# Packed biases for all keys of the second half of the queries, and copies and value products in other places, in a two-layer attention kernel

## The chip, the cores and the metric

The kernel runs on one core of a Trainium2 chip (trn2). The metric is the time of the device from the start to the end of one execution, in microseconds; several executions are timed and their median is taken.

## What is computed

Four images of 32 x 32 tokens with 768 channels pass through two layers. Both normalise over 32 groups of 24 channels, attend with 12 heads of 64 channels, project, and add the result to the input. Cut to what matters:

```python
# layer 0: every query sees all 1024 keys, with a bias by row and one by column
x = group_norm(x); q, k, v = x @ Wq + bq, x @ Wk + bk, x @ Wv + bv
attn = q @ k.T / 8
attn = attn + rel_bias_h[:, :, :, :, None] + rel_bias_w[:, :, :, None, :]
x = x + (softmax(attn) @ v) @ Wp + bp
# layer 1: every query sees its 7 x 7 neighbourhood (clipped at the borders)
x = x + neighbourhood_attention(group_norm(x), qkv_w) @ out_w
```

## The kernel before

Everything is in single precision. A matmul operand that needs it is split into a rounded part (hi) and the rest (lo), and three passes (hi by hi, hi by lo, lo by hi) stand for one product. There are eight phases f: layer 0 and layer 1 of each image. A phase projects q and k (in `project`), then v, then runs over six pairs p of heads, and ends with the output projection.

**Units.** In layer 0 a pair has 16 units u. Unit u takes the tile t = u % 8 of 128 keys and the half u // 8 of 512 queries, for both heads. `scores` issues the passes of a unit, each as two matmuls of 64 rows (head 0 on the upper half of the array, head 1 on the lower): three for q and k, then the bias. The bias is a product of a 0/1 matrix that tells each key's row and column (`onehot`, 64 lines) with the bias of each query (b_hi, then b_lo): two passes, k = 3 and k = 4. A packed unit needs one pass for both: `packed` holds of b_hi and b_lo only the lines that the keys at hand use, side by side, and `key_block` is the 0/1 matrix for it. Before the change a packed unit must lie in the upper half of the key tiles (t >= 4), and from u = 4 (6 in pair 0) or u = 12 on. Head by head the maxima of the next pair (L1327, two passes, DVE reduces them) are woven into the units. ScalarE (ACT) takes the exponential of a unit's scores into one of six `prob` slots (L828), GpSimd (POOL) adds the units up into `acc` for the denominators (L644), and TensorE (PE) multiplies prob with v (`values`, L1453), four units at a time (`GROUPED`), and sums `acc` over partitions (`sums`, L1470). `scores` of a unit waits for the exponential of the unit two before it. The order of all of it is written out by hand in each engine's program; engines meet at semaphores.

**Queue of SP.** All DMAs of the pairs are issued in one queue, in this order for a pair p > 0 of layer 0: `load_bias` for pair p + 2; `spread(p - 1, 1)`, eight DMAs that spread the reciprocals of the second half of pair p - 1 over the partitions (L491), waiting for DVE's reciprocal (L1016), which waits for ACT's copy of the sums (L734), which waits for the sums (L1470) that PE issues after unit 1; in the last pair the weights of chunk 9; `pack(p, 1)`, twelve DMAs into `packed1` (L475 and L477, four times two of rows and one of columns); `spread(p, 0)`; `pack(p + 1, 0)`, twelve DMAs into `packed0`. In pair 0 `pack(0, 0)` and `pack(0, 1)` stand behind each other when v is ready. PE waits for the twelve DMAs in front of pass k = 3 of the first packed unit of a half:

```python
if is_packed and u in PACKED_FROM[p > 0] and k == 3:
    pe.wait_ge(pack_in[half], packed_no(f, p))
```

**Layer 1.** A pair has 8 units, one for each tile of keys, over 224 to 352 queries. `values` of units 4 to 7 of the pair before come behind unit 1 and those of units 0 to 3 behind unit 5; `sums` of the pair before follow unit 3 and `shift` (L1370) of the next pair follows unit 5. ACT copies the pair's output (L728, `out_copy`) after the exponential of unit 2.

**Start.** `WARM_UP` products of ones (L1478) run before the first statistics, then PE waits for the first normalised input.

Of the kernel before, what the change touches and what calls it, by code (L numbers as in the profile page):

```python
# [33 lines left out]
ADDS = (2 * QT - 2, QT - 2)  # L34
PARTS = (2, 1)
GROUPED = 4
WARM_UP = 6
ORDER = (list(range(QT)), [0, 7, 1, 6, 2, 5, 3, 4])
P_SLOTS = 6
LAST = PAIRS - 1  # L40
# [1 line left out]
SET_LOADS = [128 + 16, 0, 128, 128]  # L42
G_SLOTS = 3
BLOCK = SIDE // 2
PACKED_FROM = ([6, 12], [4, 12])


def centre(i):
# [141 lines left out]
    return 192 * (f // 2 * PAIRS + p + 1)  # L190


def first_no(f, p):

    return f // 2 * (PAIRS + 1) + (PAIRS + 1 if f % 2 else p + 1)
# [22 lines left out]
def rows_of(h):  # L218
    return slice(64 * h, 64 * h + 64)
# [17 lines left out]
def build(nc, x_in, w_in, bqk_in, bv_in, bp_in, rel_in, onehot_src, block_in, mask_in, group_src, ident_in,  # L237
# [53 lines left out]
    for s, at in enumerate(bias_at):  # L291
# [4 lines left out]

    packed = [m.put("packed0", [128, 2, HALF], F32R, at=slot_at[0]),
              m.put("packed1", [128, 2, HALF], F32R, at=one + 40 * KB)]  # L300
    max_wide0 = m.put("max_wide0", [128, 4, 256], F32R, at=slot_at[0] + 8 * KB)

    onehot_raw = m.put("onehot_raw", [128, TOKENS], at=m.at)
# [45 lines left out]
    turned, b_first, max_mm, max_ok, col_ok, shift_mm = (sem(n) for n in (  # L349
        "turned", "b_first", "max_mm", "max_ok", "col_ok", "shift_mm"))  # L350
    half_mm, half_max_ok, wide_ok = sem("half_mm"), sem("half_max_ok"), sem("wide_ok")
    onehot_in, onehot_ok, pack_in = sem("onehot_in"), sem("onehot_ok"), sems("pack_in", 2)
    shifted, b_hi_ok, b_lo_ok = sem("shifted"), sem("b_hi_ok"), sem("b_lo_ok")
    score_ok, prob_ok, pv_done, added, acc_zero = (sem(n) for n in (
        "score_ok", "prob_ok", "pv_done", "added", "acc_zero"))
# [52 lines left out]
    with nc.Block() as block:  # L408

        @block.sync  # L410
        def _(sp):
# [24 lines left out]
            def load_bias(f, p):  # L436
                s = SET_OF[f % 2][p]
                if p == 0:
                    sp.wait_ge(gshift_ok, norm_no(f, len(norm_parts(f)) - 1))
                elif p == 1:  # L440
                    sp.wait_ge(v_mm, f * VN + 2 * QT)
                elif p > 2:
                    sp.wait_ge(score_ok, unit_no(f, p - 3, 2 * QT - 1))
                    sp.wait_ge(pack_in[1], packed_no(f, p - 3))
                else:
                    sp.wait_ge(v_mm, (f + 1) * VN)
                if f % 2:
                    sp.dma_start(b_lo_raw[s][:, :], mask_in).then_inc(bias_in[s], 16)
                    return
                sp.wait_ge(g_sent[p % G_SLOTS], 16 * (f // 2 * 2 + p // G_SLOTS + 1))  # L450
                for h in range(2):
                    for part, dst in ((0, b_lo_raw[s]), (1, b_hi_raw[s])):
                        a = 64 * h + SIDE * part
                        band = bass.AP(g_mem[p].tensor, ((p * 2 + h) * 128 + 64 * part) * TOKENS,
                                       [[TOKENS, SIDE], [TOKENS + SIDE, SIDE], [1, SIDE]])
                        sp.dma_start(dst[a:a + SIDE, :].rearrange("p (i j) -> p i j", j=SIDE), band)\
                            .then_inc(bias_in[s], 16)

            def pack(f, p, h):


                s = SET_OF[0][p]
                sp.wait_ge(b_lo_ok, f // 2 * PAIRS + p + 1)
                if p:
                    sp.wait_ge(score_ok, unit_no(f, p - 1, (h + 1) * QT - 1))
                else:
                    sp.wait_ge(v_mm, (f + 1) * VN)
                cols = slice(h * HALF, (h + 1) * HALF)
                to = packed[h][:, :, :].bitcast(F32)
                for e, part in enumerate((b_hi[s], b_lo[s])):  # L470
                    for head in range(2):
                        a, b = 64 * head, 64 * head + BLOCK * e
                        for n in range(2):
                            rows = part[a + BLOCK * n:a + BLOCK * n + BLOCK, cols].bitcast(F32)
                            sp.dma_start(to[b:b + BLOCK, n, :], rows).then_inc(pack_in[h], 16)  # L475
                        columns = part[a + SIDE:a + SIDE + BLOCK, cols].bitcast(F32)
                        sp.dma_start(to[b + SIDE:b + SIDE + BLOCK, :, :],  # L477
                                     columns.unsqueeze(1).to_broadcast([BLOCK, 2, HALF]))\
                            .then_inc(pack_in[h], 16)

            def load_onehot(f):
                sp.dma_start(onehot_raw[:, :], onehot_src[f % 2]).then_inc(onehot_in, 16)
# [21 lines left out]
            for f in range(PHASES):  # L504
# [38 lines left out]
                for p in range(PAIRS):  # L543
                    if layer == 1:
                        if p == 3:
                            if f + 1 < PHASES:
                                sp.wait_ge(bn_ok, 2 * (f + 2) * CT)
                            weights(f, 9)
                        if p == LAST and f + 1 < PHASES:
                            sp.wait_ge(shifted, pair_no(f, LAST))  # L550
                            sp.dma_start(group[:, :, :], group_src).then_inc(group_in, 16)
                        if p:
                            spread(f, p - 1, 0)
                        if p == 0:
                            next_tile(3)
                            next_tile(4)
                        if p == 1:
                            next_tile(5)
                        continue
                    if 0 < p < PAIRS - 2:  # L560
                        load_bias(f, p + 2)
                    if p:
                        spread(f, p - 1, 1)
                    if p == LAST:
                        sp.wait_ge(pack_in[1], packed_no(f, LAST - 1))
                        weights(f, 9)
                    if p:
                        pack(f, p, 1)
                    if p == LAST:
                        sp.wait_ge(score_ok, unit_no(f, LAST, QT - 1))  # L570
                        weights(f, 10)
                    spread(f, p, 0)
                    if p < LAST:
                        pack(f, p + 1, 0)
# [102 lines left out]
        def _(act):  # L677
# [74 lines left out]
            for f in range(PHASES):  # L752
# [67 lines left out]
                for p in range(PAIRS):  # L820
                    for u in range(UNITS[layer]):
# [8 lines left out]
                        if layer == 0:  # L830
# [12 lines left out]
                            if u == 9:  # L843
                                if ahead:
                                    bias_turn(f, p + 2, 1)
                                sums_copy(f, p, 0)
                            if u == 10 and ahead:
                                bias_first(f, p + 2)
                            if u == (11 if p else 13) and p < LAST:
                                widen(f, p + 1)  # L850
                            if u == 12:
                                out_copy(f, p, 0)
                            if u == (12 if p else 13) and p < LAST:
                                bias_hi(f, p + 1)
                        else:
                            if u == 2 and p:
                                out_copy(f, p - 1, 0)
                            if u == 3 and p:
                                sums_copy(f, p - 1, 0)
# [389 lines left out]
        def _(pe):  # L1249
# [126 lines left out]
            def scores(f, p, u, n=None):  # L1376
# [4 lines left out]
                keys = slice(t * 128, (t + 1) * 128)  # L1381
                ug = units_before(f, p) + u
                half = u // QT
                is_packed = layer == 0 and t >= QT // 2 and u >= PACKED_FROM[p > 0][half]
                passes = 4 if layer or is_packed else 5

                def score_pass(k, h):
                    w = (k_hi, k_hi, k_lo, None, None)[k]
                    x = (q_hi, q_lo, q_hi, b_hi[s], b_lo[s])[k]
                    if k < 3:  # L1390
                        w, x = w[rows_of(h), p, keys], x[rows_of(h), p, a:b]
                    elif is_packed:
                        w, x = key_block[rows_of(h), t % 2, :], packed[half][rows_of(h), int(t % 4 < 2), :]
# [5 lines left out]
                def bias_ready(k):  # L1399
                    if is_packed and u in PACKED_FROM[p > 0] and k == 3:  # L1400
                        pe.wait_ge(pack_in[half], packed_no(f, p))
                    if u == 0 and k == 3:
                        pe.wait_ge(shifted, pair_no(f, p))
                        if layer == 0:
                            pe.wait_ge(b_hi_ok, f // 2 * PAIRS + p + 1)
# [66 lines left out]
                sums_issued[0] += 1  # L1472


            pe.wait_ge(const_ok, 1)
            one_column = ones[:, 0:1]
            for n in range(WARM_UP):
                nc.tensor.matmul(score[:, 0, 0, :], one_column.to_broadcast([128, 128]),  # L1478
                                 one_column.to_broadcast([128, HALF]), start=True, stop=True)
            mean_averages(0, 0)  # L1480
            shift_averages(0, 0)
            for f in range(PHASES):
                layer = f % 2
                hi, lo = in_halves(f)
# [65 lines left out]
                for p in range(PAIRS):  # L1550
                    for u in range(UNITS[layer]):
                        if layer == 1:
                            scores(f, p, u)
                            if u == GROUPED + 1:
                                for e in range(GROUPED):
                                    values(f, p, e)
                            elif u == 1 and p:
                                for e in range(QT - GROUPED, QT):
                                    values(f, p - 1, e)
                            if u == 3 and p:  # L1560
                                sums(f, p - 1, 0)
                            if u == 5 and p < LAST:
# [18 lines left out]
                            sums(f, p - 1, 1)  # L1581

                last_pair = PAIRS - 1
                for u in range(UNITS[layer] - GROUPED, UNITS[layer]):
                    values(f, last_pair, u)

                def output(n, c):
# [113 lines left out]
```

## Time and profile before

| | |
|---|---|
| median of 3 runs | 3190.11 us (3186.83 to 3190.49) |
| the profiled execution, its own time | 3189.31 us |
| its span, first to last instruction | 3187.5 us |
| mean granted clock of TensorE | 0.997 |
| busy: PE, DVE, ACT, POOL | 98%, 54%, 38%, 34% |
| layer 0's pair, from its first unit to the next pair's | 42.8 us in pairs 1 to 3 |
| layer 1's pair | 12.45 us |

PE is the engine to read first, since it is nearly always busy. The table gives the length of a pair because the change works inside a pair: there are 24 of each layer.

### The profile page before, as it was taken

The page shows a single profiled execution, that of the slowest core. Times are in us where ns is not written, and L with a number is a line of the kernel's source. Part 1 is how long each engine was busy: PE and PEld are TensorE (multiplying, and loading weights), DVE is VectorE, ACT ScalarE, POOL GpSimd, SP SyncE. Part 2 cuts the span into 40 slices and gives each one's busy share as a digit, 9 for nine tenths or more (in the row PEclk, how much of TensorE's full clock was granted, in tenths as well). Part 3 has the DMA queues.
Part 4 walks back from the last instruction along what each step waited for, and adds up shares of the span by engine and source line. Part 5 has one row for each costly group of instructions (what it writes and reads, how often), then busy time and mean ns, then how long its engine had stood idle before and what let it go on. Part 6 is the DMA issues. An engine that isn't in the chain of part 4 may idle for free.

```text
span 3187.5 us, 48944 instructions
## 1 busy us (share of the span) xinstructions
PE 3113.8 (98%) x20072; PEld 2319.8 (73%) x20072; DVE 1719.5 (54%) x1921; ACT 1223.3 (38%) x1397; POOL 1086.1 (34%) x618
## 2 busy tenths in 40 slices
PE   8999999999999999999999999999999999999999
PEld 6876558887787555888778755688777875568876
DVE  4448745436435884444734588444463457744434
ACT  3345542134234654213423465321342355532132
POOL 0037860025003776003400487500430057840042
PEclk9999999999999999999999999999999999999999
DMA  3212223114321223211531222411153122141113
GB/s 128 94 39 51 47 79 116 40 57 143 133 94 32 51 46 99 98 40 65 170 123 67 40 49 43 133 69 41 63 179 109 67 47 51 38 138 60 41 34 116
DMA packets 193178, 249.38 MB, mean 78 GB/s; under 512 B 123200, under 2 KB 135872, under 8 KB 192960
## 3 DMA queue, kind: packets, MB, share of 16 engines
q1 hardware_dynamic: 191424, 244.69, 26.1%
q8 instruction: 163, 2.67, 0.4%
q10 hardware_dynamic: 1536, 1.57, 0.2%
q14 instruction: 55, 0.45, 0.0%
HBM read 145.50 MB, written 50.33 MB: 61 GB/s over the span
## 4 chain that ended last, share of the span: by engine, by line
PE 81%; ACT 5%; POOL 5%; issue 4%; DVE 3%; DMA 1%; SPq 0%; ACTq 0%; POOLq 0%
PE score L1251 14%; PE score L1252 13%; PE score L1253 13%; PE lot L1453 12%; PE score L1396 12%; PE lot L1327 8%; POOL acc L644 5%; ACT prob L828 2%; PE lot L1470 2%; DMA raw<-weights 1%; PE lot L1251 1%; PE lot L1253 1%; PE lot L1252 1%; PE lot L1370 1%; PE lot L1294 1%
## 5 line engine op out<-in xcount | busy, mean ns | idle before, releaser
L644 POOL TENSOR_TENSOR acc<-acc,prob 128x1024 f32<-128x1024 f32 x288 | 714.0, 2479 | 181.4 <-ACT prob L828 147.2
L828 ACT ACTIVATE prob<-score 128x1024 f32<-128x1024 f32 (+3 forms) x576 | 516.0, 910 | 391.6 <-PE score L1396 388.1
L974 DVE TENSOR_REDUCE max_part<-lot 128x1 f32<-128x512 f32 x640 | 412.0, 685 | 130.9 <-PE lot L1327 124.9
L1453 PE MATMUL lot<-prob,v 128*64 128x512 f32 (+4 forms) x2496 | 463.9, 515 | 8.7 <-ACT o_raw L724 7.1
L644 POOL TENSOR_TENSOR acc<-prob 128x1024 f32<-128x1024 f32 x48 | 120.1, 2503 | 833.1 <-ACT prob L828 833.1
L1396 PE MATMUL score<-q_hi,k_hi 64*128 64x512 f32 (+3 forms) x1152 | 340.7, 406 | 23.1 <-ACT prob L828 20.9
L1327 PE MATMUL lot<-k_hi,q_hi 64*128 64x512 f32 (+2 forms) x1152 | 335.7, 393 | 10.3 <-issue 5.4
L1453 PEld LDWEIGHTS lot<-prob,v 128*64 128x64 f32 x2496 | 166.9, 138 | 236.1 <-issue 197.2
L895 DVE TENSOR_TENSOR w_lo<-raw,w_hi 128x1536 fp32r<-128x1536 f32 x95 | 181.8, 1914 | 247.4 <-ACT w_hi L681 247.0
L1396 PE MATMUL score<-q_lo,k_hi 64*128 64x512 f32 (+3 forms) x1152 | 309.4, 359 | 0.0
L1396 PE MATMUL score<-q_hi,k_lo 64*128 64x512 f32 (+3 forms) x1152 | 309.1, 359 | 0.0
L662 POOL COPY acc<-prob 128x256 f32<-128x256 f32 x96 | 41.0, 428 | 752.7 <-ACT prob L828 695.6
L1327 PE MATMUL lot<-onehot,b_hi 64*128 64x512 f32 x768 | 259.4, 390 | 0.0
L681 ACT ACTIVATE w_hi<-raw 128x1536 fp32r<-128x1536 f32 x96 | 142.5, 1484 | 295.0 <-DMA raw<-weights 295.0
L1251 PE MATMUL score<-in_b,w_hi 128*128 128x512 f32 x576 | 228.3, 396 | 12.0 <-DVE in_a L951 6.4
L960 DVE TENSOR_REDUCE max_col<-lot 128x2 f32<-128x448 f32 (+1 forms) x192 | 139.7, 770 | 185.8 <-PE lot L1327 185.8
L1396 PEld LDWEIGHTS score<-q_hi,k_hi 64*128 64x128 f32 x1152 | 154.7, 184 | 114.6 <-ACT prob L828 75.2
L1327 PEld LDWEIGHTS lot<-k_hi,q_hi 64*128 64x128 f32 x1152 | 165.6, 184 | 97.0 <-issue 46.5
L1251 PE MATMUL score<-in_a,w_hi 128*128 128x512 f32 x576 | 230.0, 399 | 6.3 <-DVE q_lo L1098 4.4
L1252 PE MATMUL score<-in_b,w_hi 128*128 128x512 f32 x576 | 224.8, 390 | 0.0
L1252 PE MATMUL score<-in_a,w_hi 128*128 128x512 f32 x576 | 224.8, 390 | 0.0
L802 ACT ACTIVATE v<-score 128x256 f32<-128x256 f32 x192 | 73.9, 385 | 393.2 <-PE score L1253 393.0
(131 smaller groups left out, 7058.6 us busy)
## 6 DMA issues: line engine op xcount, KB each, us to landing
raw<-weights SPq DMA_DIRECT2D x96, 768.0 KB, 4.4
g_mem<-g SPq DMA_DIRECT2D x24, 1024.0 KB, 4.7
xin<-x_t SPq DMA_DIRECT2D x24, 512.0 KB, 6.3
xr<-x_t SPq DMA_DIRECT2D x24, 512.0 KB, 5.5
x_mem<-xr SPq DMA_DIRECT2D x24, 512.0 KB, 6.6
xr<-x_mem SPq DMA_DIRECT2D x24, 512.0 KB, 5.8
y_t<-xr SPq DMA_DIRECT2D x24, 512.0 KB, 6.9
recip<-recip SPq DMA_DIRECT2D x368, 32.0 KB, 1.9
```

What stands on the lines that cost most here:

```text
L644: nc.gpsimd.tensor_tensor(acc[:, :, a:b], with_, now, ALU.add).then_inc(added, 1)
L681: nc.scalar.activation(w_hi[c % 2][:, :, :], raw[c % 2][:, :, :], ACT.Copy).then_inc(w_hi_ok, 1)
L828: nc.scalar.activation(prob[:, ug % P_SLOTS, :, 0:b - a], score[:, u % 2, :, 0:b - a], ACT.Exp, scale=SCALE).then_inc(prob_ok, 1)
L895: nc.vector.tensor_tensor(w_lo[s][:, :, :], raw[s][:, :, :], w_hi[s][:, :, :].bitcast(F32), ALU.subtract).then_inc(w_lo_ok, 1)
L960: nc.vector.reduce_max(max_col[:, p, t, :], banks[:, :, 0:b - a], AX.X).then_inc(max_ok, 1)
L974: nc.vector.reduce_max(max_part[:, t, part, h:h + 1], lot[:, (2 * n + h) % 3, :], AX.X)\
L1251: nc.tensor.matmul(out, w[0], a[0], start=first, stop=False)
L1252: nc.tensor.matmul(out, w[0], a[1], start=False, stop=False)
L1253: return nc.tensor.matmul(out, w[1], a[0], start=False, stop=last)
L1327: return nc.tensor.matmul(lot[:, bank, 0:b - a], w, x, start=(e == 0), stop=(e == 1))
L1396: return nc.tensor.matmul(score[:, slot, h, 0:b - a], w, x, start=(k == 0), stop=(k == passes - 1))
L1453: last = nc.tensor.matmul(lot[rows_of(h), bank, x - half * HALF:y - half * HALF], v[:, t, p * 128 + 64 * h:p * 128 + 64 * h + 64], prob[:, ...
```

## The change

- In the second half of the queries of layer 0 all eight key tiles are packed units, from u = 8 on, not only the last four. `packed1` has a second plane for it, with the rows for both planes and the columns of either half of the keys, and it lies in other places (two of them, one for the last pair).
- `pack(p, 1)` issues sixteen DMAs. The first twelve are counted in `pack_in[1]`; the eight of rows write both planes (64 KB each where they wrote 32). The last four are counted in `columns_in`, for which PE waits at u = 12. The wait for `pack_in[1]` stands at u = 8 and no longer at u = 12.
- ACT: `bias_first` behind the exponential of unit 9 (it was behind 10), `out_copy(p, 0)` behind that of unit 11 (12), in layer 1 `out_copy` behind that of unit 1 (2).
- Layer 1's `values` go by two units: behind unit 1 the last two of the pair before, behind units 3, 5 and 7 two each.
- Three more products of ones behind the first statistics.

```diff
-WARM_UP = 6
+WARM_UP, REWARM = 6, 3
-PACKED_FROM = ([6, 12], [4, 12])
+PACKED_FROM = ([6, 8], [4, 8])
...
+def columns_packed_no(f, p):
+
+    return 64 * (f // 2 * PAIRS + p + 1)
...
+    packed0 = m.put("packed0", [128, 2, HALF], F32R, at=one + 40 * KB)
+    packed1 = [m.put(f"packed1{n}", [128, 2, 2, HALF], F32R, at=at)
+               for n, at in enumerate((slot_at[0], bias_at[0]))]
...
+                for part, a, b in parts:
+                    for n in range(2):
+                        rows = part[a + BLOCK * n:a + BLOCK * n + BLOCK, cols].bitcast(F32)
+                        if h:
+                            sp.dma_start(to[b:b + BLOCK, :, n, :],
+                                         rows.unsqueeze(1).to_broadcast([BLOCK, 2, HALF]))\
+                                .then_inc(pack_in[1], 16)
+                        else:
+                            sp.dma_start(to[b:b + BLOCK, n, :], rows).then_inc(pack_in[0], 16)
+                    if h:
+                        sp.dma_start(to[b + SIDE:b + SIDE + BLOCK, 0, :, :], columns(part, a, 0))\
+                            .then_inc(pack_in[1], 16)
+                    else:
+                        sp.dma_start(to[b + SIDE:b + SIDE + BLOCK, :, :], columns(part, a, 1))\
+                            .then_inc(pack_in[0], 16)
+                for part, a, b in parts if h else []:
+                    sp.dma_start(to[b + SIDE:b + SIDE + BLOCK, 1, :, :], columns(part, a, 1))\
+                        .then_inc(columns_in, 16)
...
                             if u == 9:
                                 if ahead:
                                     bias_turn(f, p + 2, 1)
+                                    bias_first(f, p + 2)
                                 sums_copy(f, p, 0)
-                            if u == 10 and ahead:
-                                bias_first(f, p + 2)
...
-                            if u == 12:
+                            if u == 11:
                                 out_copy(f, p, 0)
...
-                            if u == 2 and p:
+                            if u == 1 and p:
                                 out_copy(f, p - 1, 0)
...
-                is_packed = layer == 0 and t >= QT // 2 and u >= PACKED_FROM[p > 0][half]
+                is_packed = layer == 0 and u >= PACKED_FROM[p > 0][half]
...
+                        x = packed1[p // LAST][:, t // 4, :, :] if half else packed0[:, :, :]
+                        w, x = key_block[rows_of(h), t % 2, :], x[rows_of(h), int(t % 4 < 2), :]
...
+                    if is_packed and u == QT + QT // 2 and k == 3:
+                        pe.wait_ge(columns_in, columns_packed_no(f, p))
...
             mean_averages(0, 0)
             shift_averages(0, 0)
+            products_of_ones(REWARM)
...
-                            if u == GROUPED + 1:
-                                for e in range(GROUPED):
-                                    values(f, p, e)
+                            if u % 2 and u > 1:
+                                values(f, p, u - 3)
+                                values(f, p, u - 2)
                             elif u == 1 and p:
-                                for e in range(QT - GROUPED, QT):
-                                    values(f, p - 1, e)
+                                values(f, p - 1, QT - 2)
+                                values(f, p - 1, QT - 1)
...
-                for u in range(UNITS[layer] - GROUPED, UNITS[layer]):
+                for u in range(UNITS[layer] - (2 if layer else GROUPED), UNITS[layer]):
```

## Rows read from the trace of the kernel before

**Rows 1.** The page's busy times: busy us, share of the span, instructions.
```profile
PE 3113.8 (98%) x20072; PEld 2319.8 (73%) x20072; DVE 1719.5 (54%) x1921; ACT 1223.3 (38%) x1397; POOL 1086.1 (34%) x618
```

**Rows 2.** Timeline of PE in pair 2 of image 0: passes 3 and 4 of unit 8.
```profile
308.47 0.39 PE L1396 MATMUL score<-b_hi,onehot 64*128 64x512 f32 x1
...
308.71 0.39 PE L1396 MATMUL score<-b_lo,onehot 64*128 64x512 f32 x1
```

**Rows 3.** Timeline of the same pair, all engines, from the sums behind unit 1.
```profile
294.27 0.64 PE L1470 MATMUL lot<-acc,ones 128*32 128x256 f32 x8
...
295.39 1.75 DVE L1016 RECIPROCAL recip<-sums 128x256 f32<-128x256 f32 x1 [0.72 <-ACT sums L734]
...
297.17 4.98 SPq L491 DMA_DIRECT2D recip<-recip  x8
...
302.25 1.17 SPq L475 DMA_DIRECT2D packed<-b_hi  x2
...
309.29 0.63 SPq L477 DMA_DIRECT2D packed<-b_lo  x1
```

**Rows 4.** The tile packed over the span: min/median/max ns, first and last start.
```profile
L475 SPq DMA_DIRECT2D packed<-b_lo x192: 532/590/1751, 207.1 to 2806.3; - x192
```

**Rows 5.** DMA issues over the span: count, KB each, median us to landing.
```profile
packed<-b_lo SPq DMA_DIRECT2D x96, 64.0 KB, 2.3
```

**Rows 6.** Timeline: twelfth DMA, and pass 3 of unit 8, image 0, pair 0.
```profile
218.12 0.63 SPq L477 DMA_DIRECT2D packed<-b_lo  x1
...
218.86 0.39 PE L1396 MATMUL score<-b_hi,onehot 64*128 64x512 f32 x1
```

**Rows 7.** Timeline: the same two, image 3, pair 4.
```profile
2763.87 0.39 PE L1396 MATMUL score<-b_hi,onehot 64*128 64x512 f32 x1
...
2765.79 0.63 SPq L477 DMA_DIRECT2D packed<-b_lo  x1
```

**Rows 8.** Timeline: the same two, image 3, pair 5.
```profile
2802.41 0.40 PE L1396 MATMUL score<-b_hi,onehot 64*128 64x512 f32 x2
...
2806.91 0.63 SPq L477 DMA_DIRECT2D packed<-b_lo  x1
```

**Rows 9.** Timeline of PE, waits behind unit 8: image 0, pairs 0, 2 and 5.
```profile
238.76 0.46 PE L1327 MATMUL lot<-k_hi,q_hi 64*128 64x512 f32 x1 [1.36 <-issue]
...
320.77 0.50 PE L1396 MATMUL score<-q_hi,k_hi 64*128 64x512 f32 x2 [0.59 <-ACT prob L828]
...
439.03 0.64 PE L1470 MATMUL lot<-acc,ones 128*32 128x256 f32 x8 [1.00 <-POOL acc L644]
```

**Rows 10.** Stretches: length, busy PE, PEld, DVE, ACT, POOL, granted clock, DMA.
```profile
19.30:22.70 3.40, 2.91 (x7) 1.84 (x7) 3.37 (x8) 1.06 (x1) 0.00 (x0) 0.50 0.00 0
239.00:243.00 4.00, 3.87 (x30) 2.94 (x30) 3.22 (x5) 2.57 (x3) 1.58 (x2) 1.00 0.12 26
3118.50:3122.00 3.50, 3.50 (x22) 1.84 (x20) 3.50 (x4) 1.42 (x3) 1.55 (x1) 0.51 0.09 23
```

**Rows 11.** Timeline of PE in layer 1: units 0 and values, pairs 2 and 5.
```profile
709.25 0.37 PE L1396 MATMUL score<-q_hi,k_hi 64*128 64x224 f32 x2 [0.21 <-ACT prob L828]
...
710.48 2.38 PE L1453 MATMUL lot<-prob,v 128*64 128x320 f32 x24
712.80 0.43 PE L1396 MATMUL score<-q_hi,k_hi 64*128 64x352 f32 x2
713.07 0.32 PE L1396 MATMUL score<-q_lo,k_hi 64*128 64x352 f32 x2
...
748.57 0.37 PE L1396 MATMUL score<-q_hi,k_hi 64*128 64x224 f32 x2 [1.26 <-ACT prob L828]
749.21 4.05 PE L1453 MATMUL lot<-prob,v 128*64 128x320 f32 x24
```

**Rows 12.** Timeline of PE at the start: idle before the first projection.
```profile
19.39 0.77 PE L1251 MATMUL score<-in_b,w_hi 128*128 128x512 f32 x1 [5.83 <-DVE in_a L951]
...
22.69 0.50 PE L1251 MATMUL score<-in_b,w_hi 128*128 128x512 f32 x1 [0.41 <-DVE in_a L951]
```

More of the change, by code:

```diff
@@ L295, in build @@
         b_lo_raw.append(s != 1 and m.put(f"b_lo_raw{s}", [128, TOKENS], at=at + 4 * KB))
-    packed = [m.put("packed0", [128, 2, HALF], F32R, at=slot_at[0]),
-              m.put("packed1", [128, 2, HALF], F32R, at=one + 40 * KB)]
+    packed0 = m.put("packed0", [128, 2, HALF], F32R, at=one + 40 * KB)
+    packed1 = [m.put(f"packed1{n}", [128, 2, 2, HALF], F32R, at=at)
+               for n, at in enumerate((slot_at[0], bias_at[0]))]
     max_wide0 = m.put("max_wide0", [128, 4, 256], F32R, at=slot_at[0] + 8 * KB)
@@ L351, in build @@
     half_mm, half_max_ok, wide_ok = sem("half_mm"), sem("half_max_ok"), sem("wide_ok")
-    onehot_in, onehot_ok, pack_in = sem("onehot_in"), sem("onehot_ok"), sems("pack_in", 2)
+    onehot_in, onehot_ok = sem("onehot_in"), sem("onehot_ok")
+    pack_in, columns_in = sems("pack_in", 2), sem("columns_in")
     shifted, b_hi_ok, b_lo_ok = sem("shifted"), sem("b_hi_ok"), sem("b_lo_ok")
@@ L444, in load_bias @@
                     sp.wait_ge(pack_in[1], packed_no(f, p - 3))
+                    sp.wait_ge(columns_in, columns_packed_no(f, p - 3))
                 else:
@@ L468, in pack @@
                 cols = slice(h * HALF, (h + 1) * HALF)
[L469 to L479, printed above, removed]
+                to = (packed1[p // LAST][:, :, :, :] if h else packed0[:, :, :]).bitcast(F32)
@@ new lines, in pack, with columns @@
+                parts = [(part, 64 * head, 64 * head + BLOCK * e)
+                         for e, part in enumerate((b_hi[s], b_lo[s])) for head in range(2)]
+                def columns(part, a, keys):
+                    a += SIDE + BLOCK * (1 - keys)
+                    return part[a:a + BLOCK, cols].bitcast(F32).unsqueeze(1).to_broadcast([BLOCK, 2, HALF])
+                for part, a, b in parts:
[13 more added lines that the diff above has]
+                            .then_inc(pack_in[0], 16)
@@ L565, in _ @@
                         sp.wait_ge(pack_in[1], packed_no(f, LAST - 1))
+                        sp.wait_ge(columns_in, columns_packed_no(f, LAST - 1))
                         weights(f, 9)
@@ L1392, in score_pass @@
                     elif is_packed:
-                        w, x = key_block[rows_of(h), t % 2, :], packed[half][rows_of(h), int(t % 4 < 2), :]
+                        x = packed1[p // LAST][:, t // 4, :, :] if half else packed0[:, :, :]
+                        w, x = key_block[rows_of(h), t % 2, :], x[rows_of(h), int(t % 4 < 2), :]
                     else:
@@ L1472, in sums, with products_of_ones @@
                 sums_issued[0] += 1
+            def products_of_ones(n):
+                column = ones[:, 0:1]
+                for _ in range(n):
+                    nc.tensor.matmul(score[:, 0, 0, :], column.to_broadcast([128, 128]),
+                                     column.to_broadcast([128, HALF]), start=True, stop=True)
             pe.wait_ge(const_ok, 1)
[L1476 to L1479, printed above, removed]
+            products_of_ones(WARM_UP)
             mean_averages(0, 0)
             shift_averages(0, 0)
+            products_of_ones(REWARM)
             for f in range(PHASES):
```

## The prediction, made before the changed kernel ran

> **What bounds the kernel now.** First the page: TensorE (PE) is busy 98% of the span, the others at most 54% [rows 1]. So work taken from PE's own stream, or a wait put into it, comes out of or goes into the time almost one to one, as long as no other engine is just behind. Next I read PE's idle time behind unit 8 of layer 0: what there is comes from ACT (0.59 us before unit 12 in the pairs 1 to 3), from POOL (1.00 us in a last pair) and at a pair's start [rows 9]. Then the queue of SP, since the change moves a wait on DMAs from unit 12 to unit 8: the rows to compare are when the last of twelve `pack` DMAs is issued and when PE reaches pass 3 of unit 8. Last the clock and layer 1.
>
> **The pass taken away.** A pass is one matmul per head, and the two run side by side on the two halves of the array. Pass 3 of unit 8 starts at 308.47, pass 4 at 308.71 [rows 2], and head by head the passes follow each other at about 0.23 us. Units 8 to 11 lose pass 4: 4 x 24 pairs = 96 passes x 0.227 us = **-21.8 us**. (The matmuls go from five to four passes in 96 units, 192 matmuls fewer.)
>
> **The wait that moves.** In the shown pair the chain is: sums behind unit 1 at 294.27, ACT's copy, DVE's reciprocal at 295.39 for 1.75 us, SP's eight `spread` DMAs from 297.17 to 302.15, the twelve `pack` DMAs from 302.25 to the last one at 309.29 [rows 3]. The diff changes nothing ahead of those twelve: same copy of the sums behind unit 1, same reciprocal, same place in SP's queue. The queue is held by the issuing itself: 590 ns per DMA of rows [rows 4], and 632 ns for one with two planes (0.63 in the last line of [rows 3]). Eight DMAs of rows become two-plane ones: 8 x 0.04 = 0.33 us more. A DMA of 64 KB lands 2.3 us after its issue [rows 5]. So the twelfth has landed at 309.29 + 0.33 + 2.3 = 311.9. PE reaches pass 3 of unit 8 at 308.47 [rows 2], and nothing before it gets shorter. It stands for **3.4 us**. Before, it waited at unit 12, 11.3 us later, where all had long landed. Behind the waiting instruction lies PE's whole stream: the rest of unit 8, the woven maxima, the values, the sums. No work covers it, for PE runs in order.
>
> The same subtraction (last issue + 2.63 - pass 3) for other pairs: 1.9 us in pair 0 of image 0 [rows 6], 2765.79 + 2.63 - 2763.87 = 4.5 in pair 4 of image 3 [rows 7], and 2806.91 + 2.63 - 2802.41 = 7.1 in its last pair [rows 8]; there SP issues the weights first and PE has no maxima to pass the time with. Over all 24 pairs (first [rows 6], last [rows 8]): pair 0 gives 1.2 to 1.9, the sixteen of pairs 1 to 4 give 2.8 to 4.5 with a mean of 3.8, the last 6.2 to 7.3. Sum: 6.3 + 60.7 + 27.1 = **+94 us**. It comes again in each pair, since the chain starts anew behind each unit 1. The last four DMAs (`columns_in`) are issued 4 x 0.63 = 2.6 us later and wanted at unit 12, some 10 us later: nothing. They also push what SP does next by 2.6 us; `spread(p, 0)` comes some 10 us later in any case. If that cover were gone it would cost up to 2.6 us x 24 = 62.
>
> **The clock.** After the 5.83 us idle at the start [rows 12] the granted clock is 0.50, that is 1.2 GHz, for another 3.4 us of matmuls, and in layer 1 of image 3 it is 0.51 for 3.5 us [rows 10] behind a wait like the 1.26 us one of image 0 [rows 11]. There too: 24 matmuls of values took 4.05 us where they take 2.38 [rows 11], so a fall costs 1.7 us. Against it: behind the 1.36 us of idle at 238.76 [rows 9] the clock stayed at 1.00, 2.4 GHz [rows 10]. The stalls here lie between, 2.8 to 7.3 us in pairs 1 to 5, nearer to the one of 5.83. Bounds: 0, and 24 x 1.7 = 41. I take a fall in pairs 1 to 5 and none in pair 0: 20 x 1.7 = **+34 us**. The Trainium skill, "TensorE: Matmul & The Clock Gate", section "Why this matters for your kernels", says that idle gaps between bursts of matmuls take the clock back to half; by that rule every long stall costs its second helping, and without it the sum is 34 lower. It is the rule that speaks against this change.
>
> **ACT's moves in layer 0.** `bias_first` behind unit 9's exponential fills time in which ACT waits for the sums, so exponential 10 and then unit 12 are not held up; `out_copy` earlier frees the bank for the values behind unit 13. What there is to win is the idle behind unit 8: per image 0.5 (pair 0, without its 1.36), 3 x 0.8, 0.7 and 1.5, that is 5.1, or 20 us over the kernel [rows 9]. A PE that has just stood for 4 us no longer waits for ACT or POOL either. Bounds 0 and 20, nearer to 20: **-16 us**.
>
> **Layer 1.** Values by two make two more groups of values per pair. What a switch costs shows in part: the first pass of scores behind the values lasts 0.43 us, the next of the same shape 0.32 [rows 11]. With as much on entering and some draining I estimate 0.3 us per group. One of the new groups stands before `sums`, where a switch is made anyway: 0.55 us more per pair. In return waits go: the 0.21 before unit 0, with a restart of 0.1, and shorter unnamed ones before units 1 and 5, together 0.9 of the 12.45 us of a pair. Net -0.35 x 20 = -7. In the pair-5 start the 1.26 us wait [rows 11] shrinks by about 0.8 in four images (-3), and its falls of clock (two of four images) may go (-3). Bounds: 24 x 0.55 = +13 if no wait goes, -20 if all do. I take **-12 us** (rounded).
>
> **Start.** Three more products take 3 x 1.3 us, in an idle time of 5.83 us [rows 12]. They could hold the clock up, but PE's next wait ends at 22.69 by DVE [rows 12] and swallows it. **0**, at most -1.7.
>
> **Sum.** 3189.3 (the profiled execution's own time, span 3187.5 and 1.8 around it) + 94 + 34 - 21.8 - 16 - 12 = 3267.5. The median of the runs is 0.8 above the profiled one: **3268 us**, 2.4% slower.
>
> **The rivals.**
>
> - *The stall without the fall of the clock.* For it: 1.36 us of idle left the clock alone [rows 10]. Against: the 5.83 us did not. 3268 - 34 = 3234 us. Chance 0.20.
> - *The other side: the twelve land in time, and the kernel is faster.* One mechanism: the chain from the sums of unit 1 to the twelfth landing gets shorter than PE's way to unit 8. In the shown pair it is 311.9 - 294.3 = 17.6 us against 14.2. All of it gone: 3190.1 - 21.8 - 16 - 12 = 3140 us. It decides from where the mean stall is under (21.8 + 16 + 12) / 24 = 2.1 us, without a fall of the clock; the mean by the rows is 3.9. Nothing in the diff shortens it. Chance 0.09.
> - *Something between, stalls of 2 us.* 3184 to 3197 us. Chance 0.03.
> - *Worse than the sum:* layer 1's groups cost 13 instead of giving 12, the waits for ACT stay, and a low clock outlasts one helping. 3268 + 25 + 16 = 3309 us. Chance 0.13.
> - *As forecast,* 3250 to 3290: chance 0.55.
>
> **How the numbers follow.** The point is that of the likeliest case. The range takes the case without the fall with its terms at the good end, 3189 + 94 - 22 - 20 - 17 = 3224, and goes up to 3300, short of the worst; outside remain the faster cases and about half of the worse. About 0.2% (6 us) is what a measurement of this kernel can tell from no change: slower 0.88, same 0.03, faster 0.09.
>
> **What would show it.** In the profile after, PE waits for DMA `packed<-b_lo` (or b_hi) before pass 3 of unit 8 in each pair, about 24 times, 94 us in all, and no wait at unit 12. PE's granted clock is near 0.5 for some 3 us behind most of them, the mean clock near 0.987. The packed matmuls go from 368 to 560, those of b_lo from 400 to 208. Layer 1's pair takes 12.1 us and not 12.45. If the waits for DMA are missing, the step on SP's queue is wrong, and the time is that of the faster rival; if they are there at full clock, the second rival holds.

## The result, and the profile after

The changed kernel takes 3294.73 us (median of 4 runs, 3284.65 to 3298.25), the kernel before beside it 3190.3 (4 runs, 3186.83 to 3190.72). The ratio is 1.0325, with a 95% interval of 1.03 to 1.0349: 104 us slower, where 3268 was forecast. The profiled execution took 3296.55 us, its span is 3294.8, and its mean granted clock 0.976 (before 0.997). In the new kernel's numbering `scores` is L1422, `values` L1481, `sums` L1498, `spread` L516, and `pack` L491 and L497.

The page's busy times first, as in [rows 1]:

```profile
PE 3148.8 (96%) x19886; PEld 2321.4 (70%) x19886; DVE 1684.5 (51%) x1921; ACT 1228.8 (37%) x1397; POOL 1084.6 (33%) x618
```

PE has 186 matmul records fewer and yet is busy 35 us more, and idle 72 us more. So two things happened: it stands, and some of its work runs slower. Who made it stand is in the waits of PE after (engine, line, what for: us in total, times, longest):

```profile
PE score L1422 <- DMA packed<-b_lo: 94.6, 24, 8.1
PE score L1422 <- ACT prob L854: 11.5, 44, 0.5
```

One wait in each of the 24 pairs, always for the same DMA, 94.6 us. Before, there was no wait for that DMA in this list, and ACT's (`prob`) led it with 20.9 us. The groups of `scores`, one for each shape (count | busy us, mean ns | idle before, releaser):

```profile
L1422 PE MATMUL score<-packed,key_block 64*128 64x512 f32 x560 | 192.8, 425 | 94.6 <-DMA packed<-b_lo 94.6
...
L1422 PE MATMUL score<-b_lo,onehot 64*128 64x512 f32 x208 | 68.3, 387 | 0.0
```

The passes are the ones forecast: 192 packed matmuls more, 192 with b_lo fewer. The packed ones last 425 ns in the mean where those with b_lo last 387: 48 of them are the first behind a stall (0.79 us each in the pair below), and more run at the lower clock.

Now the pair of [rows 2] and [rows 3] again, image 0 pair 2, timeline of all engines:

```profile
302.87 0.64 PE L1498 MATMUL lot<-acc,ones 128*32 128x256 f32 x8
...
303.99 1.75 DVE L1041 RECIPROCAL recip<-sums 128x256 f32<-128x256 f32 x1 [2.16 <-ACT sums L760]
...
305.77 5.17 SPq L516 DMA_DIRECT2D recip<-recip  x8
311.04 1.29 SPq L491 DMA_DIRECT2D packed<-b_hi  x2
...
317.08 0.39 PE L1422 MATMUL score<-q_lo,k_hi 64*128 64x512 f32 x1
...
318.11 0.60 SPq L497 DMA_DIRECT2D packed<-b_lo  x1
318.75 1.23 SPq L503 DMA_DIRECT2D packed<-b_hi  x2
320.02 1.23 SPq L503 DMA_DIRECT2D packed<-b_lo  x2
320.64 0.79 PE L1422 MATMUL score<-packed,key_block 64*128 64x512 f32 x1 [3.17 <-DMA packed<-b_lo]
```

The chain is hardly longer than it was: from the sums to the last of the twelve issues 15.24 us, 15.02 before. Only its end is wanted earlier. PE comes to the pass at about 317.5 and stands until 320.64, for 3.17 us; 3.4 was forecast for this pair. The four DMAs of L503, issued behind the twelve, hold nobody up: there is no wait at unit 12. The chain that ended last, followed back from that matmul, shows the same in its last pieces (start, us, what):

```profile
317.48 0.59 SPq L491
318.07 0.04 issue
318.11 2.49 DMA packed<-b_lo
320.60 0.04 issue
320.64 0.79 PE score L1422 x2
```

Here the queue of SP is on the path that sets the end, and over the span too: the page of after gives it 11% of that chain.

Next the clock behind the stall (stretch: length, busy PE, PEld, DVE, ACT, POOL with counts, granted clock, DMA share, GB/s):

```profile
317.60:320.60 3.00, 0.00 (x0) 0.00 (x0) 0.29 (x1) 0.72 (x1) 2.86 (x2) 0.87 0.70 107
320.60:324.00 3.40, 3.36 (x16) 2.67 (x18) 1.29 (x2) 1.02 (x1) 0.67 (x1) 0.50 0.37 60
324.00:328.00 4.00, 4.00 (x17) 1.67 (x17) 3.11 (x4) 3.42 (x3) 2.37 (x1) 0.67 0.02 4
328.00:331.00 3.00, 3.00 (x24) 1.11 (x22) 1.15 (x2) 1.04 (x2) 0.00 (x0) 1.00 0.00 0
...
19.20:36.40 17.20, 16.56 (x53) 13.74 (x54) 6.55 (x14) 1.63 (x2) 0.86 (x1) 0.51 0.01 1
```

The granted clock is 1.00 in the dense work before (308.00 to 317.40), falls while PE stands, is 0.50 (1.2 GHz) for the first 3.4 us of matmuls behind it and returns within the next 4. That is what a stall leaves behind, and by the Trainium skill, "TensorE: Matmul & The Clock Gate", section "Why this matters for your kernels" (idle gaps between bursts take the clock back to half), it had to be expected; the trace agrees for 19 of the 24 stalls. The last row is something else: at the start of this run the low clock lasted from 19.2 to 36.4 us although PE was busy for 16.56 of 17.20. The first attention unit began at 205.99, where before it began at 200.20.

Last, layer 1: ACT waits in a new place, and the pass behind it too (timeline of ACT and PE, image 0):

```profile
754.64 1.06 ACT L773 ACTIVATE q_hi<-o_raw 128x1024 fp32r<-128x1024 f32 x1 [1.78 <-DVE o_raw L1047]
755.61 0.96 ACT L854 ACTIVATE prob<-score 128x448 f32<-128x448 f32 x2
...
756.18 0.43 PE L1422 MATMUL score<-q_hi,k_hi 64*128 64x352 f32 x2 [0.53 <-ACT prob L854]
```

The pair of layer 1 takes 12.04 us in pairs 1 and 2 and 12.65 in pairs 3 and 4, where it took 12.45.

### The profile page after: what moved, and what is told of

It reads as the page before. It is cut to its first block, busy times and chain, and to the rows that moved or that the text cites. A ratio compares the mean times of both kernels' runs of the same rounds, so it can differ in the third digit from the quotient of the medians.

```text
span 3294.8 us, 48680 instructions
## 1 busy us (share of the span) xinstructions
PE 3148.8 (96%) x19886; PEld 2321.4 (70%) x19886; DVE 1684.5 (51%) x1921; ACT 1228.8 (37%) x1397; POOL 1084.6 (33%) x618
## 4 chain that ended last, share of the span: by engine, by line
PE 71%; SPq 11%; DVE 5%; issue 4%; DMA 4%; ACT 2%; POOL 2%; ACTq 0%; POOLq 0%; DVEq 0%
PE score L1276 15%; PE score L1277 13%; PE score L1278 13%; PE lot L1481 9%; PE score L1422 8%; PE lot L1352 7%; SPq L516 4%; SPq L491 4%; DMA packed<-b_lo 2%; POOL acc L670 2%; DVE recip L1041 2%; SPq L497 1%; PE lot L1498 1%; PE lot L1395 1%; DMA raw<-weights 1%
## 5 line engine op out<-in xcount | busy, mean ns | idle before, releaser
L1481 PE MATMUL lot<-prob,v 128*64 128x512 f32 (+4 forms) x2496 | 478.7, 521 | 1.6 <-ACT prob L854 1.6
L1352 PE MATMUL lot<-k_hi,q_hi 64*128 64x512 f32 (+2 forms) x1152 | 346.6, 404 | 9.6 <-issue 5.4
L1422 PE MATMUL score<-q_hi,k_hi 64*128 64x512 f32 (+3 forms) x1152 | 340.1, 406 | 13.4 <-ACT prob L854 11.5
L1481 PEld LDWEIGHTS lot<-prob,v 128*64 128x64 f32 x2496 | 158.7, 138 | 243.3 <-issue 194.8
L920 DVE TENSOR_TENSOR w_lo<-raw,w_hi 128x1536 fp32r<-128x1536 f32 x95 | 173.8, 1830 | 299.8 <-ACT w_hi L707 299.7
L1422 PE MATMUL score<-q_hi,k_lo 64*128 64x512 f32 (+3 forms) x1152 | 319.5, 372 | 0.0
L1422 PE MATMUL score<-q_lo,k_hi 64*128 64x512 f32 (+3 forms) x1152 | 314.6, 368 | 0.0
L1422 PE MATMUL score<-packed,key_block 64*128 64x512 f32 x560 | 192.8, 425 | 94.6 <-DMA packed<-b_lo 94.6
L1352 PE MATMUL lot<-onehot,b_hi 64*128 64x512 f32 x768 | 270.8, 411 | 0.0
L1352 PEld LDWEIGHTS lot<-k_hi,q_hi 64*128 64x128 f32 x1152 | 174.9, 192 | 97.0 <-issue 45.4
L1276 PE MATMUL score<-in_b,w_hi 128*128 128x512 f32 x576 | 229.6, 399 | 8.1 <-DVE q_lo L1119 5.6
L1422 PEld LDWEIGHTS score<-q_hi,k_hi 64*128 64x128 f32 x1152 | 158.9, 188 | 104.0 <-ACT prob L854 57.2
L1278 PE MATMUL score<-in_b,w_lo 128*128 128x512 f32 x576 | 226.1, 392 | 0.0
```

The costliest lines, as they stand in the source:

```text
L920: nc.vector.tensor_tensor(w_lo[s][:, :, :], raw[s][:, :, :], w_hi[s][:, :, :].bitcast(F32), ALU.subtract).then_inc(w_lo_ok, 1)
L1276: nc.tensor.matmul(out, w[0], a[0], start=first, stop=False)
L1278: return nc.tensor.matmul(out, w[1], a[0], start=False, stop=last)
L1352: return nc.tensor.matmul(lot[:, bank, 0:b - a], w, x, start=(e == 0), stop=(e == 1))
L1422: return nc.tensor.matmul(score[:, slot, h, 0:b - a], w, x, start=(k == 0), stop=(k == passes - 1))
L1481: last = nc.tensor.matmul(lot[rows_of(h), bank, x - half * HALF:y - half * HALF], v[:, t, p * 128 + 64 * h:p * 128 + 64 * h + 64], prob[:, ...
```

## The experiments

The theory: the time is set by the wait at unit 8 for the chain of SP's queue, and by the clock that falls behind it; all else is a small gain. The rival: it is the packed passes themselves, the wider DMAs, or the values by two that are slow.

### The change with unit 12, or unit 10, as the first packed one

```diff
-PACKED_FROM = ([6, 8], [4, 8])
+PACKED_FROM = ([6, 12], [4, 12])
```

> The changed kernel with the packed units of the second half from unit 12 on, as before the change; the sixteen DMAs, their sizes, ScalarE's moves, layer 1 by two and the three products stay. Theory (the wait at unit 8): the 94.6 us of waits for DMA, some 17 us of stopping and starting again (0.7 us at each of 24 stalls) and some 30 us of low clock go, the 21.8 us of saved passes come back: 3294.7 - 94.6 - 17 - 30 + 22 = 3175 us, no wait for DMA in front of a packed pass. Rival (the larger and additional DMAs, or the moves of ScalarE and of layer 1, are what costs): it stays above 3250.

Measured: 3175.08 us (5 runs, 3174.22 to 3178.41; before beside it 3189.59), ratio 0.9959 (0.9945 to 0.9973), clock 0.998, no wait for `packed<-b_lo`. All sixteen DMAs, the two planes, ACT's moves, layer 1 and the start are in it. So nothing of these is slow; all of the loss, and more, comes with packing units 8 to 11.

```diff
-PACKED_FROM = ([6, 8], [4, 8])
+PACKED_FROM = ([6, 10], [4, 10])
```

> The changed kernel with the packed units of the second half from unit 10 on. Unit 10 comes some 7 us behind unit 8 (values and sums of the first half lie between), and the twelve transfers land 2.8 to 4.5 us behind pass 3 of unit 8 (7.1 in the last pair, where unit 10 is 8 us behind). Theory: no stall, and half of the saved passes, 48 x 0.227 = 11 us, so 11 us under the kernel with packed units from 12: near 3164. Rival (a stall of a few tenths is left in the last pairs, clock falls there): 3170 to 3185.

Measured: 3168.32 us (4 runs, 3163.55 to 3173.11), ratio 0.9931 (0.9914 to 0.9949), clock 0.996. The groups by shape:

```profile
L1422 PE MATMUL score<-packed,key_block 64*128 64x512 f32 x464 | 150.7, 395 | 0.1
```

96 packed matmuls more than with unit 12, and 0.1 us idle before them instead of 94.6. Two units later the same DMAs have landed. The gain over unit 12 is 6.8 us against 48 passes x 0.227 = 10.9, with intervals that overlap; the pair went from 42.13 to 41.7 us, which is 0.43 of the 0.45 that two passes are worth.

### Work in place of the stall

PE issues products of ones in front of unit 8: one in pair 0, eight in the last pair, four in the others. They are added work, and nothing uses what they compute.

```diff
+                if layer == 0 and u == QT:
+                    products_of_ones(1 if p == 0 else 8 if p == LAST else 4)
```

> The changed kernel with idle work put in front of unit 8: products of ones into the scores' free banks, 4 of them in pairs 1 to 4, 8 in the last pair, 1 in pair 0, 0.85 us each at full clock (3.4, 6.8 and 0.85 us). They fill the time in which TensorE would stand, and change nothing else. Theory (the stall costs twice, by itself and by the fall of the clock behind it): waits for DMA fall to some 15 us, the time falls by the some 30 us of low clock: 3265. Rival (the clock falls anyway, or the loss behind the stall is something else): 3290 or more.

Measured: 3254.89 us (4 runs, 3253.57 to 3255.82), ratio 1.0202 (1.0187 to 1.0218), clock 0.996. The same place of image 0 pair 2, PE's timeline and then the stretches:

```profile
312.12 3.71 PE L1509 MATMUL score<-ones 128*128 128x512 f32 x8
```

```profile
308.00:316.00 8.00, 8.00 (x40) 4.09 (x38) 4.30 (x5) 2.88 (x4) 7.57 (x4) 1.00 0.66 103
316.00:320.00 4.00, 4.00 (x32) 2.63 (x32) 3.11 (x5) 2.17 (x3) 0.95 (x2) 1.00 0.33 55
```

PE loses as much time in front of the pass as it did (3.7 us of useless products where it stood 3.17 here; over the 24 pairs the way from unit 7 to unit 8 is 90 us longer than with unit 12 as the first packed one, and 2.9 us of waits are left, against 94.6), and the kernel is still 39.8 us faster than the changed one. The clock is at 1.00 in these stretches. This separates the stall from what it leaves behind. Of the 40.8 us between the two spans, 3.9 are the start (the first attention unit begins at 202.12 here), so some 37 lie in the pairs. 30 were expected, for the clock alone; the rest is put down to stopping, below.

### The twelve DMAs ahead of the spreading of the reciprocals

`spread(p - 1, 1)` goes behind the twelve, ahead of the last four. What used the spread reciprocals on DVE and ACT moves back by some units.

```diff
+                if p and h:
+                    spread(f, p - 1, 1)
                 for part, a, b in parts if h else []:
...
-                    if p:
-                        spread(f, p - 1, 1)
                     if p == LAST:
...
-                            if u == 7 and p:
+                            if u == 10 and p:
                                 out_hi(f, p - 1, 1)
...
-                        if u == 5 and p:
-                            normalise(f, p - 1, 1)
                         if u == 9 and p:
+                            normalise(f, p - 1, 1)
                             out_lo(f, p - 1, 0)
+                        if u == 11 and p:
                             out_lo(f, p - 1, 1)
```

> The changed kernel with the first twelve transfers of pack(p, 1) in SP's queue ahead of the eight of spread(p - 1, 1), which stand between them and the last four; so that nobody waits for the later spread, its multiplication on VectorE moves from unit 5 to unit 9, and the roundings behind it from 7 to 10 and from 9 to 11. Packed from unit 8 on as in the changed kernel. Theory (it is SP's queue with its 5 us of spread and the chain of sums, copy and reciprocal ahead of it): pack starts some 6 us earlier, the stalls of pairs 1 to 4 go, 1 to 2 us stay in the last pair and all of pair 0's: waits for DMA under 15 us, time 3175 - 22 + 15 to 20, near 3170. Rival (the transfers themselves are slow): waits stay over 60 us and the time over 3240.

Measured: 3178.1 us (10 runs, 3170.83 to 3185.28), ratio 0.9963 (0.995 to 0.9976), clock 0.996. PE's waits:

```profile
PE score L1422 <- ACT prob L854: 21.2, 48, 2.0
PE score L1422 <- DMA packed<-b_lo: 9.2, 7, 1.9
```

and SP's queue in image 0 pair 2, where PE issues the sums at 292.69:

```profile
295.51 2.21 SPq L491 DMA_DIRECT2D packed<-b_hi  x2
...
303.50 0.59 SPq L497 DMA_DIRECT2D packed<-b_lo  x1
304.19 4.99 SPq L518 DMA_DIRECT2D recip<-recip  x8
```

The packing starts 2.8 us behind the sums and not 8.2 us, since neither the reciprocal nor its eight DMAs stand in front. All packed passes and all DMAs of the change are in this kernel, and it is 117 us faster. So the order in SP's queue, not the number of passes or the width of the DMAs, made the wait. Left are 9.2 us in pairs 0 and 5, and new waits for ACT of 1.4 to 2.0 us before unit 13 of the last pair. There the later multiplication on DVE stands behind the splitting of weights, ACT's rounding waits for it, and the exponential stands behind the rounding (timeline of ACT, image 3):

```profile
2802.78 0.72 ACT L770 ACTIVATE q_hi<-o_raw,bv 128x512 fp32r<-128x512 f32 x1 [1.55 <-DVE o_raw L1047]
2803.41 1.01 ACT L854 ACTIVATE prob<-score 128x1024 f32<-128x1024 f32 x1
```

It does not beat unit 10: the pairs 1 to 3 take 41.7 us in both, although two more passes a pair are gone here, and the first and the last pair are longer here.

### The small parts, each alone on the kernel before

Three more products of ones at the start:

```diff
             mean_averages(0, 0)
             shift_averages(0, 0)
+            products_of_ones(REWARM)
```

> The kernel before with the three more products of ones behind the first statistics alone. In the profile of the changed kernel the low clock of the start lasted until 36.4 us instead of 22.7, and the first unit of attention came 5.8 us later than before. Theory 1 (it is where the clock happens to fall, not the products): no difference, within 2 us. Theory 2 (the three products set it off): 3 to 6 us slower. Theory 3 (they hold the clock up): up to 1.7 us faster.

Measured: 3186.92 us (12 runs, 3184.15 to 3196.36; before 3188.69 in 31 runs), ratio 0.9997 (0.9987 to 1.0006). The granted clock was 1.00 from 19.2 to 36.4 us here and 0.90 before, and the first attention unit began at 200.18 in place of 200.20: the clock was gained and swallowed by the wait for DVE, as forecast.

The values of layer 1 by two, with ACT's copy one unit earlier:

```diff
-                            if u == GROUPED + 1:
-                                for e in range(GROUPED):
-                                    values(f, p, e)
+                            if u % 2 and u > 1:
+                                values(f, p, u - 3)
+                                values(f, p, u - 2)
```

> The kernel before with layer 1's values by two and its output copy behind unit 1's exponential alone. The prediction: 12 us faster. What the profile of the changed kernel shows in the layer 1 of image 0: pairs of 12.04 us instead of 12.45 between pairs 1 and 3, but 12.65 between pairs 3 and 5, and a first pair of 10.08 instead of 9.32, in sum nothing; against it stand the waits of 1.26 us and the falls of the clock behind them, which are gone. Theory by these rows: 2 to 6 us faster.

Measured: 3182.95 us (11 runs, 3181.21 to 3185.26), ratio 0.9982 (0.9974 to 0.9991), that is -5.7 us. ACT's waits, by what it waits with and for:

```profile
ACT q_hi L747 <- DVE o_raw L1022: 26.7, 14, 3.6
```

In the groups of the kernel before, the same instruction waits 17.1 us for DVE. ACT rounds the output of an earlier pair behind the exponential of unit 7, DVE is not yet done with it, and the next exponentials stand behind it in ACT's order. Therefore this part was also tried with that rounding moved behind the first exponential of the next pair:

```diff
-                            if u == 7 and p >= 2:
+                            if u == 0 and p >= 3:
+                                out_hi(f, p - 3, 0)
+                            if u == 7 and p == LAST:
                                 out_hi(f, p - 2, 0)
```

> The kernel before with layer 1's values by two as in e5_two, and layer 1's rounding of the finished output (ScalarE, behind unit 7, where it waits for VectorE's multiplication and holds up the exponentials of the next pair: 1.78 us of idle in the changed kernel) moved behind the exponential of unit 0 of the next pair. Theory (that wait is why the pairs 3 and 4 take 12.65 us and not 12.04): 0.6 us x 2 to 3 pairs x 4 images = 5 to 7 us faster than e5_two. Rival (GpSimd's adding, some 11 us of a pair, is the next bound): within 2 us of e5_two.

Measured: 3180.69 us (11 runs, 3177.21 to 3184.33), ratio 0.9976 (0.9967 to 0.9985). The long pairs went from 12.65 to 12.13 us, as expected, but the whole is 2.3 us better with intervals that overlap, less than the 5 to 7 expected. In the profiled execution two pairs in each of four images gain 0.5 us, 4 us in all, and one of them, in image 2, took 14.11 us and gave 2 of these back; why it did is open. The place is shown by the pairs; the size in the total is not.

ACT's two moves in layer 0:

```diff
                                     bias_turn(f, p + 2, 1)
+                                    bias_first(f, p + 2)
                                 sums_copy(f, p, 0)
-                            if u == 10 and ahead:
-                                bias_first(f, p + 2)
...
-                            if u == 12:
+                            if u == 11:
                                 out_copy(f, p, 0)
```

> The kernel before with ScalarE's moves in layer 0 alone (the bias's first rounding behind unit 9, the output copy behind unit 11). The waits of 0.59 and 0.20 us behind unit 12 shrink to 0.2 in pairs 1 to 3, half as much in pair 4: 12 x 0.65 + 8 x 0.35 = 10 us faster. Rival (the waits go but turn up elsewhere, the 16 us of the prediction were TensorE's rest behind the stall): within 3 us of before.

Measured: 3178.58 us (9 runs, 3175.36 to 3183.51), ratio 0.9974 (0.9962 to 0.9986), that is -10.1 us; the pair took 42.1 and not 42.8 us.

### What the runs point to

Unit 10 as the first packed one, without the products at the start, and the rounding in layer 1 moved as above.

> Packed units of the second half from unit 10 on (e2_from10), layer 1's later rounding (e9_l1fix), without the three products at the start. Theory (the gains lie in different stages and add up): e2_from10 measured 21 us under the kernel before, e9_l1fix 2 us under e5_two: 23 to 25 us under the kernel before, near 3165. Rival (layer 1's move and the clock's falls cancel it): no better than e2_from10.

Measured: 3159.68 us (5 runs, 3156.47 to 3162.37; before 3185.4 in 9 runs), ratio 0.9914 (0.9901 to 0.9928). It beats both kernels, by 25.7 us and by about 135 us. Against unit 10 alone (0.9931) the intervals overlap, so what the last two edits add is not settled.

## Why the prediction was right, and where its terms were off

The direction, the place and the two large terms held. The time lies 27 us above the point and 5 below the upper end of the range, and nearly all the terms that were off were off to the same side. The terms against what was measured, for the profiled execution (span 3294.8 - 3187.5 = 107.3 us more):

| step | forecast | measured | from |
|---|---|---|---|
| passes taken away | -21.8 | about -21 | counts 560 and 208; 0.43 us a pair where two passes should give 0.45, unit 12 to unit 10 |
| the wait that moves | +94 | +94.6 | PE's waits |
| the clock behind it | +34 | +30 | below |
| stopping and starting again | not in the sum | +17 | below |
| the start | 0 | +5.8 | first attention unit 205.99 against 200.20 |
| ACT's moves | -16 | -10 | that part alone, on the kernel before |
| layer 1 by two | -12 | -6 | that part alone, on the kernel before |

With 21 the measured terms make 110, some 3 more than the span shows; I did not find these.

**The wait.** The subtraction (twelfth issue, its landing, minus PE's arrival) gave 1.2 to 1.9 us in pair 0, 2.8 to 4.5 in pairs 1 to 4 and 6.2 to 7.3 in pair 5. The trace has 0.77 to 2.53, 2.92 to 4.58 and 7.21 to 8.11; in sum 6.0, 57.9 and 30.7 where 6.3, 60.7 and 27.1 were forecast. So the method is good to some 10% by kind of pair, and that the sums agree within 1 us is partly luck. It is this good because nothing ahead of the twelve changed, which rested on reading SP's queue in order. The faster rival, that they land in time, had nothing in the diff to make it so; it took a change of the queue's order (the run with the twelve first) to bring it about, and then it came.

**The clock and the stop.** PE's way from unit 8 to unit 12 is 11.3 us before (10.3 in the last pair). Less 0.91 for four passes and plus the pair's own wait, what remains in the changed kernel is 0.7 us in the five pairs whose clock stayed, and 1.6 to 3.2 in the nineteen where it fell; 47 us over the 24. Against the run with unit 12 first, in which all other edits are, the same sum gives 47 too. Taking 24 x 0.7 = 17 as the cost of any stop leaves 30 for the clock, that is about 1.6 for each fall where 1.7 was forecast. That these agree is partly luck: by the trace's clock PE worked for 2.9 to 6.0 us behind a stall at 0.50, 4.5 in the mean, where the forecast had 3.4, and lost less in each of them. The mean clock was 0.976 accordingly and not 0.987. It fell in nearly all of pairs 1 to 5 and in pair 0 only once: the threefold evidence [rows 9, 10, 11] was weighed rightly, and the rival without a fall (3234) is out. The 17 us are what the sum had no term for, though its paragraph on layer 1 priced entering and draining at 0.3 us a group. Part of it can be seen: in pair 0 of image 0 (timeline of PE)

```profile
224.66 0.39 PE L1422 MATMUL score<-q_lo,k_hi 64*128 64x512 f32 x1
226.49 0.49 PE L1422 MATMUL score<-packed,key_block 64*128 64x512 f32 x1 [1.44 <-DMA packed<-b_lo]
226.49 0.50 PE L1422 MATMUL score<-q_hi,k_lo 64*128 64x512 f32 x1
226.82 0.39 PE L1352 MATMUL lot<-k_hi,q_hi 64*128 64x512 f32 x1
```

In the stream a matmul is followed after 0.23 us; here the profile counts its 0.39 us as busy and the idle time only from there (0.16 us more), and the first behind the pause is followed after 0.33 (0.10 more). So an idle of 1.44 us costs 1.70. The Trainium skill, "TensorE: Matmul & The Clock Gate", section "Single matmul latency", gives, for one bf16 matmul on the full array, 398 cycles of 2.4 GHz beyond the columns, an estimate of 0.17 us. The 0.16 here lies near it, but does not confirm it: the matmuls here are of single precision on half the rows, and their ends are modelled in the profile. The other 0.4 of the 0.7 is spread over the units behind and I could not assign it. That the clock and the stop together cost 47 us is shown by the difference to the run with unit 12 first. With products in place of the stall 37 of them went; some 9 us are still there between units 8 and 12, and why is open. How the 47 divide into clock and stop is worked out, not shown.

**The start.** The term 0 is right for what the change does: the same products alone on the kernel before changed nothing. The 5.8 us in the profiled execution go with a low clock that lasted 17 us. The five profiled kernels with these products that are told of above began their first attention unit at 200.2 to 202.1, so it is not the products as such; why the clock stayed low in this execution is open.

**ACT's moves.** All idle behind unit 8, 20 us, was counted as winnable, and 16 taken. 10 came: 0.67 us in each of the pairs 1 to 3 are 8 of them, and all other pairs together gave 2. The first of these rows is of the kernel before, the others are with ACT's moves alone:

```profile
PE lot L1453 <- ACT o_raw L724: 7.1, 24, 0.6
...
PE score L1395 <- ACT prob L828: 15.7, 56, 1.3
PE lot L1469 <- POOL acc L644: 8.6, 12, 1.1
```

The wait of the values for ACT's output copy (`o_raw`) is gone with the earlier copy, and the kernel before has 20.9 for `prob` and 4.7 in 7 places for POOL: 12 us of waiting for ACT went, and 4 of waiting for POOL, of the kind of the 1.00 us in [rows 9], came. There the next engine is just behind.

**Layer 1.** The wait before unit 0 did shrink and the pair took 12.04 us, 0.4 less, as forecast, but only in pairs 1 and 2; the first pair took 10.08 where it had taken 9.32. In pairs 3 and 4 the exponentials come earlier than DVE's output is ready, ACT waits for it within its own order, and the pair takes 12.65. The forecast asked which wait would go and not which would be next: I had read PE's idle times there, but not what ACT does between two exponentials. A slip besides: the parts of the term, 7, 3 and 3, add up to 13 and not to 12.

## What to carry to other kernels

When a wait is moved to an earlier instruction, compare two times of one pair of the trace before: when the last issue of what it waits for leaves its queue (plus its landing), and when the waiting engine comes by; what stands ahead in that queue counts in full. In this kernel a stall of TensorE cost the idle time, about 0.7 us for stopping, and 0.9 to 2.5 us more (1.6 in the mean) where the clock fell behind it; even useless products in its place gave 37 of 142 us back. And look for the place at which the transfer has just landed: two units later half of the saving was to be had, with no wait.

## What the runs showed of the hardware that was not expected

- The clock can stay low under dense work: 0.51 over 17.2 us with PE busy for 16.56 of them, at the start of one execution. Behind the stall shown above it was back in less than 8 us, and with nearly the same kernel (unit 12 as the first packed one) the same stretch of the start had 1.00.
- Stalls of much the same length had both outcomes. In pair 0 those of 0.77, 1.29 and 1.44 us left the clock alone and the one of 2.53 us did not. In pairs 1 to 4, with 2.92 to 4.58 us, it fell in fourteen of sixteen; it stayed behind one of 3.36 us and fell behind the one of 2.92.
- SP issues at nearly the same pace whether a DMA writes 32 or 64 KB: L491 (64 KB) takes 594 to 602 ns at the median, where the 32 KB ones of the other half take 590 and its 64 KB ones 632. So what counted in front of the wait was the number of DMAs, about 0.63 us each with what lies between.
